# First layer of a four-layer gated network: ternary weights made during the routed experts, one stage from gather to transposed rows, and sums over partitions on TensorE

## Chip, core and metric

The kernel runs on one core of one Trainium2 chip. The metric is the device time of one execution in microseconds (us). Three executions of the kernel before took 3488.2, 3493.2 and 3496.24 us; the median is 3493.2 us.

## What is computed

Four layers, each an attention-like part and a feed-forward part, both added to the rows x (2048 tokens of 512 numbers) behind a layer norm and a tanh gate. The change touches layer 0 and two sums in layer 2's feed-forward part:

```python
# layer 0, "xattn": each token goes to one of four experts by its id; the context rows are the experts' weights
out = where(expert_ids == e, (silu(h @ Wg[e].T) * (h @ Wu[e].T)) @ Wd[e].T, out)
x = x + tanh(g_xattn[0]) * out
# layer 0, ffn on _layernorm(x); for each of W_up, W_gate, W_down (2048x512 or 512x2048):
scale = mean(abs(w)) + 1e-8
q = clip(round(w / scale), -1, 1) * scale
x = x + tanh(g_ffn[0]) * ((silu(h @ wu.T) * (h @ wg.T)) @ wd.T)
# layer 2, ffn: per-tensor fp8 scale of the rows and of the hidden values
scale_x = maximum(max(abs(x2d)) / 448, 1e-6)
```

All three expert matrices are the same context rows here, so a tile needs two products, one with the turned context for gate and up together and one for down.

## The kernel before

The kernel is a sequence of stages (`stage`). In a stage each engine runs its own instruction list in order, the order in which it is written, and waits on semaphores that other engines or DMAs raise; a stage ends with all of its engines at a barrier. Nothing overlaps across a stage's end but DMAs that nobody waits for. P is 128 partitions, T is 16 row tiles of 128 tokens, D is 512, F is 2048, A (`ROUTED`) is 19.

Layer 0 runs through these stages:

1. `routed_context` turns the context into `cT` (fp16 high and low parts), sorts the tokens by expert into 19 tiles of 128 and starts the first four gathers of x rows.
2. `experts`, loops over the 19 tiles (a or i). Per tile: GpSimd gathers 128 rows of x (L482) into a ring of four; VectorE takes statistics (L647, L649, L651), GpSimd the root (L533), VectorE normalises (L658), ScalarE and VectorE split into fp16 high and low parts (L619, L663); TensorE turns them (L568), VectorE copies them out of PSUM (L670); TensorE multiplies by the context (L578, 12 matmuls); ScalarE silu (L628), VectorE product (L693), ScalarE high part (L632), GpSimd low part (L538); TensorE turns (L587), VectorE copies (L677, `copy_hidden`), TensorE multiplies again (L596, 12 matmuls), ScalarE scales the result (L640) and SP stores it to `expert_rows` in DRAM (L521). SP has issued the load of all of x (4 MB) and the store of `cT` (4 MB) at the start. GpSimd's order in step i is root(i+3), low part(i), gather(i+4). VectorE's is `copy_rows`(i+1), product(i), normalise(i+2), statistics(i+3), low part(i+2), `copy_hidden`(i-1). After the last tile GpSimd gathers the 16 tiles of results back in token order (L555) and VectorE adds them to x (L707).
3. `ternary_matrices`: 12 slabs of 1 MB (four of each matrix) are loaded (L743); VectorE sums absolute values (L759, then L765, L766), GpSimd adds over the partitions with `partition_all_reduce` (L750), VectorE makes the step size (L772 to L774), ScalarE scales and rounds to int32 (L816), VectorE clips to -1..1 in fp16 (L780), TensorE turns (L806), ScalarE copies to the matrices (L827, L830).
4. `scaled_gate`: one VectorE multiplication (L2921), a stage of its own.
5. `transposed_parts`: statistics of all 16 tiles (L159, L162, L164), roots (L172), then per tile normalise (L261), high part (L228), low part on GpSimd (L239), turn (L248), copy (L267).
6. `ternary_ffn`, whose first matmul is at L918. It prepares the matrices of later layers beside its matmuls and isn't changed.

Layer 2's feed-forward part: `fp8_rows` finds the largest absolute value of the normalised rows (L2384 per partition), GpSimd takes the maximum over partitions (L2371), and VectorE makes the scale (L2341 on). `fp8_ffn` does its first product once to find the largest hidden value (L2513, L2516, L2517), again with a GpSimd maximum (L2494), and VectorE makes the scale (L2521 to L2523); GpSimd then forms a root with `pow` (L2497) and a product (L2499), and only after that ScalarE starts on the second pass (L2484).

Of the kernel before, what the change touches and what calls it, by code (L numbers as in the profile page):

```python
# [25 lines left out]
P = 128  # L26
D = 512
# [459 lines left out]
def experts(k, cT, rows, rows_loaded, tokens, places, weights_of):  # L487
# [4 lines left out]
    UP, ROWS, HIDDEN, Y = (0, 1), 2, 3, (4, 5)  # L492
    YR, GR = 3, 8
    with stage(k, "x_loaded", "context_stored", "stats_ready", "mv_ready", "var_ready", "power_ready", "rstd_ready", "normal_ready",
               "hi_ready", "parts_ready", "rows_turned", "rows_copied", "up_ready", "silu_ready", "prod_ready",
               "hid_hi_ready", "hid_ready", "hid_turned", "hid_copied", "down_ready", "y_ready", "stored0", "stored1",
               "stored2", "got0", "got1", "got2", "got3", "got4", "got5", "got6", "got7", "added") as s:
        stored = (s.stored0, s.stored1, s.stored2)
        got = (s.got0, s.got1, s.got2, s.got3, s.got4, s.got5, s.got6, s.got7)
# [13 lines left out]
        got_y = s.sb("got_y", [P, GR, D], F32)  # L513

        @s.block.sync
        def _(sp):
            sp.dma_start(k.x[:], k.x_in.rearrange("(t p) d -> p t d", p=P)).then_inc(s.x_loaded, 16)
            sp.dma_start(k.context_parts, cT[:].rearrange("p l c n -> p (l c n)")).then_inc(s.context_stored, 16)
            for a in range(A):
                sp.wait_ge(s.y_ready, a + 1)  # L520
                sp.dma_start(k.expert_rows[cols(a, P), :], y[:, a % YR, :]).then_inc(stored[a % YR], 16)  # L521
            sp.wait_ge(s.context_stored, 16)

        @s.block.gpsimd
        def _(pool):
            pool.memset(power[:], -0.5).then_inc(s.power_ready, 1)
# [23 lines left out]
            for u in range(YR):  # L550
                pool.wait_ge(stored[u], 16 * len(range(u, A, YR)))
            for t in range(T):
                if t >= GR:
                    pool.wait_ge(s.added, t - GR + 1)
                pool.indirect_dma_start(out=got_y[:, t % GR, :], out_offset=None, in_=k.expert_rows,  # L555
                                        in_offset=bass.IndirectOffsetOnAxis(ap=places[:, t:t + 1], axis=0)
                                        ).then_inc(got[t % GR], 16)

        @s.block.tensor
        def _(pe):  # L560
# [38 lines left out]

            turn_rows(0)  # L600
# [11 lines left out]
        def _(act):  # L612
# [7 lines left out]

            high(0)
            high(1)
            for i in range(A + 2):
# [9 lines left out]
                if i + 2 < A:  # L633
                    high(i + 2)
# [2478 lines left out]
```

## Time and profile before

| | us |
|---|---|
| executions shown | 3488.2, 3493.2, 3496.24 |
| profiled execution, its own time | 3497.81 |
| its span | 3496.1 |
| mean granted TensorE clock | 0.89 of full |

| engine | busy us | share |
|---|---|---|
| TensorE matmul | 2737.5 | 78% |
| TensorE weight load | 1414.9 | 40% |
| VectorE | 2564.6 | 73% |
| ScalarE | 1847.2 | 53% |
| GpSimd | 715.6 | 20% |

The shares are means over some forty stages with different limits. The change is in the stages between 44 and 329 us and at two points near 2816 and 2921 us, so the lines of the trace there are read, not the shares.

### The profile page before, as it was taken

What the parts mean: (1) busy time and instruction counts of PE and PEld (TensorE: products, weight loads), DVE (VectorE), ACT (ScalarE), POOL (GpSimd) and SP (SyncE); (2) the same over time, 40 slices, a digit from 0 to 9 for tenths busy, and PEclk for the clock granted to TensorE, in tenths of its full rate; (3) what the DMA queues carried; (4) which work ended last, traced back from release to release, by engine and by line L of the source; (5) the groups of instructions that cost most, each with busy time, mean ns of one, the idle gap of its engine ahead of it and who ended that gap; (6) DMA issues with size and microseconds to landing.
All of it is one profiled execution on the core that took longest, in us unless ns stands there. A gap on an engine that the chain in (4) does not pass through costs nothing. (4 is left out here: it accounts for less than half of the span.)

```text
span 3496.1 us, 63537 instructions
## 1 busy us (share of the span) xinstructions
PE 2737.5 (78%) x21394; PEld 1414.9 (40%) x21394; DVE 2564.6 (73%) x4744; ACT 1847.2 (53%) x2674; POOL 715.6 (20%) x610
## 2 busy tenths in 40 slices
PE   5925999776799999999996677786788647758983
PEld 3413444333365656565663433343111323224541
DVE  5555667575799999999994666524699787986548
ACT  2324433233399999999992533322587222434551
POOL 4422000022101010010104233303012603550013
PEclk8965999897899999999998898897999769978996
DMA  5261431200000000000000200100331100023301
GB/s 172 73 207 49 145 103 61 100 0 16 18 8 12 13 7 13 7 13 7 7 1 15 85 0 0 58 17 13 85 78 32 55 15 1 0 66 65 65 6 53
DMA packets 65285, 151.90 MB, mean 43 GB/s; under 512 B 11793, under 2 KB 20001, under 8 KB 63329
## 3 DMA queue, kind: packets, MB, share of 16 engines
q1 hardware_dynamic: 62320, 140.43, 13.4%
q0 software_dynamic: 2800, 9.18, 0.9%
q8 instruction: 116, 1.90, 0.2%
q14 instruction: 49, 0.39, 0.0%
HBM read 93.61 MB, written 24.38 MB: 34 GB/s over the span
## 5 line engine op out<-in xcount | busy, mean ns | idle before, releaser
L1527 DVE TENSOR_REDUCE s_top<-ps 128x1 f32<-128x512 f32 x1024 | 657.4, 684 | 31.1 <-PE ps L1422 30.8
L1496 ACT ACTIVATE s_prob<-ps,s_shift,m_sq 128x1024 int16<-128x1024 f32 x512 | 614.7, 1201 | 30.6 <-DVE s_shift L1535 30.4
L1422 PE MATMUL ps<-s_ks,s_qs 128*128 128x512 f16 x1024 | 352.2, 385 | 62.3 <-issue 14.8
L1427 PEld LDWEIGHTS ps<-ident,s_prob 128*128 128x128 f16 x4096 | 272.5, 98 | 123.3 <-DVE m_o L1545 53.7
L1427 PE MATMUL ps<-ident,s_prob 128*128 128x128 f16 x4096 | 313.9, 220 | 0.7 <-ACT s_prob L1496 0.5
L1415 PE MATMUL ps<-s_ks,s_qs 128*128 128x512 f16 x1024 | 306.6, 381 | 0.7 <-ACT s_prob L1496 0.5
L1502 ACT ACTIVATE s_probT<-ps 128x1024 f16<-128x1024 int16 x256 | 261.9, 1023 | 5.6 <-PE ps L1427 5.1
L248 PE MATMUL ps<-ident,s_parts 128*128 128x128 f16 x768 | 93.3, 297 | 151.5 <-POOL s_parts L239 149.4
L1540 DVE CAST s_probT<-ps 128x1024 f16<-128x1024 int16 x256 | 174.4, 681 | 3.9 <-PE ps L1427 3.9
L2199 DVE TENSOR_SCALAR s_prob<-ps,s_cap 128x1024 f32<-128x1024 f32 x128 | 158.2, 1270 | 24.6 <-PE ps L2108 24.6
L1406 POOL TENSOR_TENSOR s_sums<-s_z 128x16 f32<-128x16 f32 x16 | 3.5, 217 | 835.5 <-DVE m_o L1545 835.5
L2804 DVE TENSOR_REDUCE s_ntop<-ps 128x1 f32<-128x512 f32 (+3 forms) x256 | 107.5, 484 | 86.7 <-PE ps L2664 86.7
L2143 ACT ACTIVATE s_prob<-s_prob 128x1024 f32<-128x1024 f32 x128 | 131.1, 1051 | 58.5 <-DVE s_prob L2199 55.5
L969 ACT ACTIVATE s_silu<-ps,scale 128x512 f32<-128x512 f32 x64 | 43.9, 685 | 206.8 <-PE ps L918 206.8
L1422 PEld LDWEIGHTS ps<-s_ks,s_qs 128*128 (+1 forms) x1024 | 80.2, 96 | 169.3 <-DVE s_top L1527 108.6
L2122 PE MATMUL ps<-s_prob,m_values 128*32 128x512 f32 x512 | 136.0, 610 | 12.8 <-ACT s_prob L2143 12.6
L1435 PE MATMUL ps<-s_hv,s_probT 128*128 128x32 f16 x4096 | 142.3, 176 | 1.7 <-ACT s_probT L1502 1.7
L228 ACT ACTIVATE s_parts<-s_rows 128x512 f16<-128x512 f32 x80 | 49.0, 627 | 178.1 <-DVE s_rows L261 150.2
L248 PEld LDWEIGHTS ps<-ident,s_parts 128*128 128x128 f16 x768 | 69.4, 134 | 177.7 <-POOL s_parts L239 177.7
L2125 PE MATMUL ps<-s_prob,s_ones 128*32 128x512 f32 x512 | 136.0, 610 | 0.0
L2775 ACT ACTIVATE s_prob<-ps 128x384 f32<-128x384 f32 (+1 forms) x192 | 89.6, 516 | 85.8 <-PE ps L2687 85.6
L1435 PEld LDWEIGHTS ps<-s_hv,s_probT 128*128 128x128 f16 x4096 | 129.5, 96 | 2.2 <-issue 2.2
(384 smaller groups left out, 6020.1 us busy)
## 6 DMA issues: line engine op xcount, KB each, us to landing
s_qs<-m_qT SPq DMA_DIRECT2D x144, 128.0 KB, 2.5
s_ks<-m_kT SPq DMA_DIRECT2D x96, 128.0 KB, 2.5
numbers<-s_numbers SPq DMA_DIRECT2D x21, 512.0 KB, 3.0
s_slabs<-numbers SPq DMA_DIRECT2D x21, 512.0 KB, 5.8
m_ks<-context_parts SPq DMA_DIRECT2D x12, 512.0 KB, 7.7
expert_rows<-s_y SPq DMA_DIRECT2D x19, 256.0 KB, 2.0
s_rows_in<-in_ctx SPq DMA_DIRECT2D x16, 256.0 KB, 3.0
x_sb<-in_x SPq DMA_DIRECT2D x1, 4096.0 KB, 14.4
```

The lines of the kernel that those rows point to most:

```text
L248: t = pe.transpose(k.ps16[:, u, cols(m, P)], parts[:, u, m // DC, cols(m % DC, P)], k.ident[:])
L1415: j = pe.matmul(pair(half)[:, m, :], qs[:, hb, bass.ds(t * P, P)], ks[:, hb, cols(2 * half + m, 512)], start=True, stop=True)
L1422: pe.matmul(quarter_at(q), qs[:, hb, bass.ds(t * P, P)], ks[:, hb, cols(q, 512)], start=True, stop=True).then_inc(s.top_scored, 1)
L1427: j = pe.transpose(turned(half, F16)[:, cols(m, P)], prob[:, u, cols(8 * half + m, P)].bitcast(F16), k.ident[:])
L1435: j = pe.matmul(output, probT[:, u, m, :], hv[:, hb, m, :], start=(m == 0), stop=(m == T - 1))
L1496: act.activation(prob[:, u, cols(half, HALF)], pair(half).rearrange("p m n -> p (m n)"), ACT.Exp, bias=shift[:, u:u + 1], scale=sq[:, bass ...
L1502: act.activation(probT[:, u, 8:16, :].rearrange("p m n -> p (m n)"), turned(1, I16), ACT.Copy).then_inc(s.half1_copied, 1)
L1527: dve.tensor_reduce(top4[:, u, q:q + 1], quarter_at(q), AX.X, ALU.max).then_inc(s.top_read, 1)
L1540: dve.tensor_copy(probT[:, u, 0:8, :].rearrange("p m n -> p (m n)"), turned(0, I16)).then_inc(s.half0_copied, 1)
L2122: pe.matmul(values_at(m)[cols(j, HD), :], values[:, b * KT + t, 2 * pair + j, :], prob[:, n % R, j, :], start=(t == 0), stop=(t == KT - 1))
L2125: i = pe.matmul(sums_at(m)[cols(j, HD), :], ones[:], prob[:, n % R, j, :], start=(t == 0), stop=(t == KT - 1))
L2199: dve.tensor_scalar(prob[:, n % R, :, :], k.ps[:, 2 * (n % A):2 * (n % A) + 2, :], cap[:, tile:tile + 1], -LIMIT, ALU.min, ALU.max).then_i ...
```

## The change

- `ternary_matrices` and `scaled_gate` are removed. The slabs are loaded, summed, scaled and clipped inside `experts`, into the tile `numbers` (fp16, not yet turned). x isn't loaded in `experts` any more: its place in memory and that of the later `hT` hold the slabs.
- In `experts` SP issues two slab loads in each of steps 0 to 2 and one in each of steps 7 to 12, and the store of `cT` in step 13. VectorE gets `clip`(i-7) and `absolute`(i-2) at the end of a step; ScalarE gets `multiply`(i-6) and takes `copy_hidden` over from VectorE, both at fixed places in its order. The sum over partitions is a matmul with a matrix of ones.
- Gathering back, adding, statistics, normalising and turning of the rows become one stage `expert_rows_added`, which works tile by tile, with the turning of the weights on TensorE and ScalarE in between. x is loaded there, in four pieces. Normalising moves from VectorE to ScalarE, the low part from GpSimd to VectorE.
- In `fp8_rows` and `fp8_ffn` the GpSimd maximum over partitions is replaced: VectorE spreads the column over 128 columns, TensorE turns it with an fp32 matmul by the identity, VectorE reduces the 128 columns. The sums in `ternary_ffn` stay on GpSimd.

In `experts`, SP's order:

```diff
-            sp.dma_start(k.x[:], k.x_in.rearrange("(t p) d -> p t d", p=P)).then_inc(s.x_loaded, 16)
-            sp.dma_start(k.context_parts, cT[:].rearrange("p l c n -> p (l c n)")).then_inc(s.context_stored, 16)
-            for a in range(A):
-                sp.wait_ge(s.y_ready, a + 1)
-                sp.dma_start(k.expert_rows[cols(a, P), :], y[:, a % YR, :]).then_inc(stored[a % YR], 16)
+            for i in range(A + 2):
+                if 1 <= i < A:
+                    sp.wait_ge(s.up_ready, i)
+                if i < NATS // 2:
+                    load(2 * i)
+                    load(2 * i + 1)
+                if NATS <= i - 1 < LAST:
+                    sp.wait_ge(s.scaled, i - NATS)
+                    load(i - 1)
+                if i == LAST + 1:
+                    sp.dma_start(k.context_parts, cT.rearrange("p l c n -> p (l c n)")).then_inc(s.context_stored, 16)
+                if i >= 2:
+                    sp.wait_ge(s.y_ready, i - 1)
+                    sp.dma_start(k.expert_rows[cols(i - 2, P), :], y[:, (i - 2) % YR, :]).then_inc(stored[(i - 2) % YR], 16)
```

TensorE's step (`add_up` waits for `sum_ready` and is a matmul of ones by one fp32 column) and ScalarE's step:

```diff
                 if i < A:
                     up(i)
+                if i % SLABS == 2 and 0 <= i // SLABS - 1 < M:
+                    add_up(i // SLABS - 1)
...
                 if i + 2 < A:
                     high(i + 2)
+                if 0 <= i - 6 < LAST:
+                    multiply(i - 6)
...
+                if 0 <= i - 1 < A:
+                    copy_hidden(i - 1)
```

VectorE's step, behind product(i) and again behind low(i+2):

```diff
+                if i % SLABS == 2 and 0 <= i // SLABS - 1 < M:
+                    step_size(i // SLABS - 1)
...
-                if 0 <= i - 1:
-                    copy_hidden(i - 1)
+                if 0 <= i - 7 < LAST:
+                    clip(i - 7)
+                if 0 <= i - 2 < LAST:
+                    absolute(i - 2)
+                if i % SLABS == 1 and 0 <= i // SLABS - 1 < M:
+                    partial_sum(i // SLABS - 1)
```

The new stage `expert_rows_added` (all lines are new; `GR` is 8, `R` is 4), GpSimd:

```python
            for t in range(GR):
                gather(t)
            pool.memset(power[:], -0.5).then_inc(s.power_ready, 1)
            pool.wait_ge(s.power_ready, 1)
            for t in range(T):
                pool.wait_ge(s.var_ready, t + 1)
                pool.tensor_tensor(k.rstd[:, t:t + 1], var[:, t:t + 1], power[:], ALU.pow).then_inc(s.rstd_ready, 1)
                if t + GR < T:
                    pool.wait_ge(s.added, t + 1)
                    gather(t + GR)
```

VectorE (`offset_of` waits for `rstd_ready`, `low` for `hi_ready`, `copy` for `turned`):

```python
            for t in range(T + 4):
                if t < T:
                    add(t)
                if 0 <= t - 3 < T:
                    low(t - 3)
                if t < T:
                    dve.wait_ge(s.added, t + 1)
                    dve.bn_stats(bn[:, t, :], k.x[:, t, :]).then_inc(s.stats_ready, 1)
                if 0 <= t - 4:
                    copy(t - 4)
                if 0 <= t - 1 < T:
                    offset_of(t - 1)
                if t < T:
                    dve.wait_ge(s.stats_ready, t + 1)
                    dve.bn_aggr(k.mv[:, t, :], bn[:, t, :]).then_inc(s.mv_ready, 1)
                    dve.wait_ge(s.mv_ready, t + 1)
                    dve.tensor_scalar(var[:, t:t + 1], k.mv[:, t, 1:2], LN_EPS, None, ALU.add).then_inc(s.var_ready, 1)
```

TensorE turns eight banks of weights (`turn_weights_of(0)`), then one bank and one tile of rows per step; ScalarE:

```python
            copy_weights_of(0)
            for t in range(T):
                copy_weights_of(t + 1)
                act.wait_ge(s.offset_ready, t + 1)
                if t >= R:
                    act.wait_ge(s.parts_ready, t - R + 1)
                act.activation(normal[:, t % R, :], k.x[:, t, :], ACT.Identity, bias=offset[:, t:t + 1],
                               scale=k.rstd[:, t:t + 1]).then_inc(s.normal_ready, 1)
                if t >= R:
                    act.wait_ge(s.turned, t - R + 1)
                act.wait_ge(s.normal_ready, t + 1)
                act.activation(parts[:, t % R, 0, :], normal[:, t % R, :], ACT.Copy).then_inc(s.hi_ready, 1)
```

In `fp8_rows` (in `fp8_ffn` the same with bank 7):

```diff
-            pool.partition_all_reduce(total[:], top[:], P, RMAX).then_inc(s.total_ready, 1)
...
+            dve.tensor_copy(wide_top[:], top[:].broadcast_to([P, P])).then_inc(s.spread, 1)
+            dve.wait_ge(s.total_ready, 1)
+            v.done(dve.tensor_reduce(total[:], k.ps[:, 3, 0:P], AX.X, ALU.max))
...
+            pe.wait_ge(s.spread, 1)
+            pe.matmul(k.ps[:, 3, 0:P], wide_top[:], k.ident32[:], start=True, stop=True).then_inc(s.total_ready, 1)
```

## Rows read from the trace of the kernel before

**Rows 1.** Experts' stretch: length; PE, PEld, DVE, ACT, POOL busy; clock; DMA share, GB/s

```profile
44.00:194.00 150.00, 126.53 (x760) 63.01 (x760) 76.51 (x152) 47.80 (x77) 53.57 (x54) 0.93 0.32 115
```

**Rows 2.** Timeline of one tile's round: start, duration, engine, line; [idle before <-releaser]

```profile
132.43 0.69 DVE L647 BATCH_NORM_STATS2 s_bn<-m_rows 128x6 f32<-128x512 f32 x1 [2.60 <-DMA m_rows<-in_x,m_tokens]
...
133.62 0.94 POOL L533 TENSOR_TENSOR s_rstd_e<-s_var_e,s_power 128x1 f32<-128x1 f32 x1 [3.52 <-DVE s_var_e L651]
...
135.86 1.00 POOL L482 DMA_INDIRECT m_rows<-in_x,m_tokens  x1 [0.17 <-issue]
...
139.26 0.69 DVE L647 BATCH_NORM_STATS2 s_bn<-m_rows 128x6 f32<-128x512 f32 x1 [1.52 <-DMA m_rows<-in_x,m_tokens]
```

**Rows 3.** Waits of the experts' stage (44 to 194 us): total, times, longest

```profile
DVE s_bn L647 <- DMA m_rows<-in_x,m_tokens: 43.3, 15, 5.6
```

**Rows 4.** Timeline: a gather beside two 4 MB transfers, and the last tile's statistics

```profile
62.61 1.01 POOL L482 DMA_INDIRECT m_rows<-in_x,m_tokens  x1 [0.16 <-issue]
...
69.00 0.69 DVE L647 BATCH_NORM_STATS2 s_bn<-m_rows 128x6 f32<-128x512 f32 x1 [5.61 <-DMA m_rows<-in_x,m_tokens]
...
168.01 0.69 DVE L647 BATCH_NORM_STATS2 s_bn<-m_rows 128x6 f32<-128x512 f32 x1 [3.08 <-DMA m_rows<-in_x,m_tokens]
```

**Rows 5.** Groups of instructions of the operations that move: count, busy, mean ns

```profile
L759 DVE TENSOR_REDUCE s_part<-m_nat 128x32 f32<-128x2048 f32 x12 | 27.4, 2279 | 9.4 <-DMA m_nat<-in_L_ffn_W_up 9.4
L780 DVE TENSOR_SCALAR s_tern<-s_whole 128x2048 f16<-128x2048 int32 x12 | 14.7, 1222 | 10.1 <-ACT s_whole L816 10.1
L816 ACT ACTIVATE s_whole<-m_nat,s_inv 128x2048 int32<-128x2048 f32 x12 | 24.0, 2010 | 49.3 <-DVE s_inv L774 49.3
L827 ACT ACTIVATE m_w_down<-ps 128x1024 f16<-128x1024 f16 x8 | 7.8, 1038 | 0.6 <-PE ps L806 0.6
L2271 ACT ACTIVATE s_norm<-s_delta,s_offset_d,s_factor_d 128x512 f32<-128x512 f32 x16 | 13.0, 814 | 39.7 <-DVE s_offset_d L2315 39.7
```

**Rows 6.** Timeline: TensorE at half clock, back to back at full clock, and after a gap

```profile
51.66 5.30 PE L578 MATMUL ps<-m_cT,s_hT 128*128 x12 [1.50 <-DVE s_hT L670]
...
127.43 0.62 PE L568 MATMUL ps<-ident,s_parts 128*128 128x128 f16 x8 [1.78 <-DVE s_parts L663]
128.03 4.45 PE L596 MATMUL ps<-m_cT,s_hidT 128*128 x12
...
135.80 2.75 PE L596 MATMUL ps<-m_cT,s_hidT 128*128 x12
...
141.88 2.75 PE L596 MATMUL ps<-m_cT,s_hidT 128*128 x12
```

**Rows 7.** Timeline: a VectorE operation that meets a GpSimd operation

```profile
172.46 1.16 POOL L538 TENSOR_TENSOR s_hid<-s_prod,s_hid 128x512 f16<-128x512 f32 x1 [1.19 <-ACT s_hid L632]
...
172.93 1.23 DVE L663 TENSOR_TENSOR s_parts<-s_normal,s_parts 128x512 f16<-128x512 f32 x1 [0.76 <-ACT s_parts L619]
```

**Rows 8.** Timeline: last result scaled, first and last gather back

```profile
192.86 0.69 ACT L640 ACTIVATE s_y<-ps,gate 128x512 f32<-128x512 f32 x1 [3.31 <-PE ps L596]
...
195.84 1.00 POOL L555 DMA_INDIRECT s_got_y<-expert_rows,m_places  x1 [10.34 <-DMA expert_rows<-s_y]
...
216.60 1.13 POOL L555 DMA_INDIRECT s_got_y<-expert_rows,m_places  x1 [0.30 <-issue]
```

**Rows 9.** Timeline: last copy of the turned rows, then the first matmul of `ternary_ffn`

```profile
327.09 0.69 DVE L267 COPY m_hT<-ps 128x1024 f16<-128x1024 f16 x1 [0.42 <-PE ps L248]
329.03 0.14 PEld L918 LDWEIGHTS ps<-m_hT,m_w_up 128*128 128x128 f16 x2 [2.25 <-DMA m_nat<-in_L_ffn_W_up]
```

**Rows 10.** Timeline in `fp8_ffn`: maximum found, scale found, GpSimd's root

```profile
2920.72 0.15 DVE L2517 TENSOR_SCALAR s_top<-s_top 128x1 f32<-128x1 f32 x1
...
2921.86 0.15 DVE L2523 TENSOR_SCALAR s_sh<-s_total 128x1 f32<-128x1 f32 x1
...
2928.41 0.59 POOL L2497 TENSOR_TENSOR s_root<-s_sh,s_power 128x1 f32<-128x1 f32 x1 [7.05 <-issue]
```

**Rows 11.** One line's durations, fp32 matmul by the identity (min/median/max ns)

```profile
L2871 PE MATMUL ps<-ident,s_ws_col x8: 421/421/581, 3457.1 to 3458.7; 128*128 128x128 f32 x8
```

More of the change, by code:

```diff
@@ L549, in _ @@
                     gather_rows(k, pool, rows, rows_loaded, tokens, i + ROWS_RING)
[L550 to L557, printed above, removed]
         @s.block.tensor
@@ L598, in down, with add_up @@
                 i.then_inc(s.down_ready, 1)
+            def add_up(m):
+                if m == 0:
+                    pe.wait_ge(s.ones_ready, 1)
+                pe.wait_ge(s.sum_ready, m + 1)
+                pe.matmul(k.ps[:, TOTAL, m:m + 1], ones[:], sums[:, m:m + 1], start=True, stop=True).then_inc(s.total_ready, 1)
             turn_rows(0)
@@ new lines, in turn_rows @@
+            def turn_rows(t):
+                pe.wait_ge(s.parts_ready, t + 1)
+                if t >= R:
+                    pe.wait_ge(s.copied, t - R + 1)
+                for m in range(2 * DC):
+                    i = pe.transpose(k.ps16[:, t % R, cols(m, P)], parts[:, t % R, m // DC, cols(m % DC, P)], k.ident[:])
+                i.then_inc(s.turned, 1)
+            turn_weights_of(0)
+            for t in range(T + 3):
+                if t < T:
+                    turn_weights_of(t + 1)
+                if t >= 3:
+                    turn_rows(t - 3)
@@ L2424, in fp8_ffn @@
 def fp8_ffn(k, xT, wfc, wproj, sx, sfc, sproj, gate):
-    with stage(k, "vsteps", "first_ready", "first_used", "max_ready", "total_ready", "scale_ready", "root_ready",
+    with stage(k, "vsteps", "first_ready", "first_used", "max_ready", "spread", "total_ready", "scale_ready", "root_ready",
                "power_ready", "a_ready", "relu_ready", "square_ready", "magic_ready", "sum_ready", "hid_ready",
@@ L2458, in _ @@
             pe.wait_ge(s.first_used, G * FC)
+            pe.wait_ge(s.spread, 1)
+            pe.matmul(k.ps[:, 7, 0:P], wide_top[:], k.ident32[:], start=True, stop=True).then_inc(s.total_ready, 1)
             with pe.Fori(0, G) as g:
@@ L2913, in _ @@
                     dve.tensor_tensor(x, x, y[:, u, :], ALU.add).then_inc(s.x_ready, 1)
-def scaled_gate(k, out, gate, scale):
-    with stage(k, "unused") as s:
-        @s.block.vector
-        def _(dve):
-            dve.tensor_tensor(out, k.gate[:, gate:gate + 1], scale, ALU.mult)
 def gated_layers(nc, inputs, out):
@@ L2971, in layer0_ffn @@
+        cT = wide[:, 0:2, :].rearrange("p l (c n) -> p l c n", c=DC)
         with memory(k) as sb2:
-            nats = [sb2("nat%d" % m, [P, F * D // P], F32) for m in range(2)]
-            ternary_matrices(k, matrices, k.scale, 0.0, 1e-8, nats)
-        scaled_gate(k, factor[:], 4, k.scale[:, 2:3])
-        hT = sb("hT", [P, 2, DC, N], F16)
-        transposed_parts(k, hT)
+            numbers = sb2("numbers", [P, 3 * SLABS_OF, SLAB], F16)
+            places = sb2("places", [P, T], I32)
+            with memory(k) as sb3:
+                rows = sb3("rows", [P, ROWS_RING, D], F32)
+                tokens = sb3("tokens", [P, ROUTED], I32)
+                weights_of = sb3("weights_of", [P, ROUTED], I32)
+                rows_loaded = [k.nc.alloc_semaphore("expert_rows_loaded%d" % u) for u in range(ROWS_RING)]
+                routed_context(k, cT, rows, rows_loaded, tokens, places, weights_of)
+                experts(k, cT, rows, rows_loaded, tokens, weights_of,
+                        (k.i.L0_ffn_W_up, k.i.L0_ffn_W_gate, k.i.L0_ffn_W_down), k.scale, numbers, hT)
+            expert_rows_added(k, places, hT, w, numbers, factor[:], k.scale[:, 2:3])
```

307 lines of the change are left out of this document (161 added, 146 removed).

## Prediction

> **What bounds the kernel now.** The change sits in layer 0 and at two points of layer 2's feed-forward part, so the timeline there is what matters, not the page's shares. Stages don't overlap; what is saved in one comes off the end, and four lengths have to be forecast.
>
> I read the experts' stage first. TensorE is busy 126.5 of 150 us and VectorE 76.5, which is 4.03 us of VectorE for each of 19 tiles [rows 1]. TensorE looks like the bound, but at full clock two of its products lie 6.08 us apart (135.80 to 141.88) [rows 6], while the statistics of tiles 4 and 18 start at 69.00 and 168.01: 14 rounds, 7.07 us each [rows 4]. The waits say why: VectorE sat 43.3 us, 15 times, for gathered rows [rows 3]. One round runs 132.43 statistics, 133.62 root on GpSimd, its low part, 135.86 gather issued, 139.26 next statistics: 6.83 us [rows 2]. This loop of VectorE, GpSimd and DMA sets the pace. VectorE's 2.9 us of waiting a tile (43.3/15) is the room for the new work; what counts is what the new work does to the loop.
>
> Behind it, the gather back starts at 195.84, 2.3 us after the last result (192.86 + 0.69) [rows 8], and the next matmul stage starts at 329.03 [rows 9]. From last result to first matmul: 135.5 us, in which the experts' engines do nothing but wait for one another.
>
> **Part 1: from the last result to the first matmul.** Removed are the gather back, `ternary_matrices`, `scaled_gate` and `transposed_parts`, 135.5 us. In their place: store and stage change, 2.3 + about 1.2 us, where the 1.2 is the stage change of [rows 9] (327.09 + 0.69 to 329.03 is 1.25), so 3.5; the new stage; another 1.25.
>
> The new stage step by step. GpSimd issues eight gathers before its first root. The 16 of before started at 195.84 to 216.60, 1.38 us apart [rows 8]: 11.1 us, then constant and root, about 1.4 (root 0.94 [rows 2]). VectorE's second step waits for it: 13 us in. x's four loads and the gathers are hidden beside that and are needed one after the other. Steps 2 and 3 are held by GpSimd, root 0.94, gather 1.00 and gaps of 0.17 to 0.3: 2.3 us each, 4.6. Then VectorE sets the pace: four wide and three small operations. In [rows 1, 2] six wide and two small ones fill 4.03 us though each wide one lasts 0.69, so a wide one costs about 0.6 and a small one about 0.17: 2.9 us, times 12, is 35. ScalarE has a bank copy 1.04, normalising 0.81 as L2271 [rows 5], and a high part of 0.6 (512 wide like the others, an estimate): 2.5 us, under it. TensorE turns 16 blocks a step; its half clock costs 0.11 us a block (12 wide products took 5.30 at half clock, a block is a quarter of one) [rows 6]: 1.8 us. GpSimd needs 2.3 until step 7. The drain of three more steps, with one high part, low part, turn and copy in a row, is 5. Sum 13 + 4.6 + 35 + 5 = 57.6, I take 58, between 55 and 68 (ScalarE's 2.5 with 0.8 us of round trips added in every step). Together 62.8 against 135.5: **72.7 us saved**, 63 to 76.
>
> **Part 2: the experts' stage gets longer.** VectorE loses `copy_hidden` (0.69) and gains a clip of 1.22 and a sum of 2.28 [rows 5]: 4.03 + 2.81 = 6.84 us a tile, just under 7.07. ScalarE, 47.8/19 = 2.5 us, gains a multiplication of 2.01 and a copy of 1.04 [rows 1, 5]: 5.6, covered. The sums in one pass are covered by the wait for rows. What isn't covered touches the loop:
>
> The clip (tiles 0 to 11, steps 7 to 18, gathers in steps 7 to 14) is issued just when GpSimd has the low part to make. In [rows 7] VectorE's operation, no wider than L647's of 0.69, began at 172.93 inside GpSimd's 172.46 to 173.62 and took 1.23: it waited for GpSimd to end. One of the two waits: if GpSimd does, the loop grows by the clip's 1.22 less the gap; if VectorE does, its 6.84 grows by 1.16. I take 1.15 us in eight steps, 9.2; bounds 0 and 13.
>
> The loads: six slabs of 1 MB in steps 7 to 12 are issued after the store of a result, as the gather is. A gather alone takes from 135.86 to 139.26, 3.4 us; the one issued at 62.61, with 8 MB in flight, 6.4 [rows 2, 4]. So 0 to 3.0 us a gather; a slab alone is less than 8 MB, I take 1.5, six times 9. The store of `cT` (4 MB), moved from the start to step 13, meets two gathers at 3.0 each, 6. The start gains nothing: four slabs are in flight when that gather at 62.61 is issued.
>
> The two partial sums and step sizes on VectorE's path cost about 0.5 us three times, the copy on ScalarE in the tail 0.35 twice: 2.2. Sum 9.2 + 9 + 6 + 2.2 = **26 us longer**; bounds 3, and 45 if each loop pays the full 3.0 and TensorE's clock falls too.
>
> Two rules of the Trainium skill speak to this part. Its page "SBUF — State Buffer", section "Who interferes with whom", says that a VectorE operation in a two-port mode and a GpSimd operation block each other fully and that `tensor_reduce` never does, and that a gather's descriptors are written by GpSimd through the same port. By it the clip costs up to 1.22 us a step and the sum nothing; [rows 7] shows the same lock with another operation. Its page "DMA: Bandwidth & Descriptors", section "Queues, rings and completion order", says each DMA engine takes turns between queues packet by packet. By that rule a gather would get half of the engines beside a load and lose well under the 3.0 us of [rows 4]; the six loads would then cost about 5 us and not 9.
>
> **Part 3: the two maxima.** In `fp8_ffn` the scale was ready at 2921.86 + 0.15, yet the root began at 2928.41, after 7.05 us of waiting for nothing that the trace shows, right behind the GpSimd maximum [rows 10]. Everywhere else a root follows its input in a few tenths (0.17 at 133.62) [rows 2]. I read this as the price of going from the special reduction back to ordinary code. Without it: spread copy 0.3, fp32 matmul 0.6 to 0.8 with its load (0.42 alone [rows 11]), reduction 0.3, three small steps 0.6, so the root starts about 2.2 us after 2920.87 in place of 7.5: 5.3 saved, and ScalarE's whole second pass moves with it. In `fp8_rows` the new way costs about 0.9 more and nothing waits for the old code. Together **4.4 us saved**; if the gap stays, 2 lost.
>
> The Trainium skill, page "GPSIMD Engine Reference", section "Instruction dispatch", says that the first call to freshly loaded GpSimd code pays about 6 us without an instruction in the profile; by that figure the saving would be 4.3 and not 5.3.
>
> **Rivals.** *A, the loop hides it all.* GpSimd wins the port and loads slip between gathers; the experts' stage grows by 5 us. For it: 2.9 us of waiting a tile. Against it: [rows 4, 7]. 21 us less than the forecast: 3421. *B, TensorE's clock falls in many tiles.* A TensorE wait of 1.78 us stood ahead of a product of 4.45 us in place of 2.75 [rows 6]; longer rounds make such waits the rule. 1.7 us in eleven tiles is 19: 3461. *C, slower than before.* The same taken to its end: TensorE stays at 1.2 GHz, two products of 5.30 and 16 turned blocks make a step of about 12.3 us (2 × 5.3 + 16 × 0.11). Over 19 tiles that is 100 us more, less the 77 saved: 3516. It decides from about 15 such tiles. Against it: a busier TensorE regained its clock in the next tile (135.80) [rows 6]. *D, the new stage doesn't pipeline.* Variance, root, offset, normalising, high part, low part form one chain; if it costs 4.2 us a tile, the stage has 20 us more: 3462. Against it: `low` trails by three steps and `copy` by four.
>
> **How the numbers follow.** -72.7 + 26 - 4.4 = -51 us. The profiled execution took 3497.8 us (span 3496.1), 4.6 above the median of the runs, so the difference is taken off the median: 3493.2 - 51 = 3442. Chances: forecast 0.51, A 0.22, B 0.13, D 0.08, C 0.04, no difference 0.02. A measurement can tell about 0.2%, 7 us. The range goes from A less 6 us of Part 1 to B and D plus 9: 3415 to 3470. Faster 0.94, same 0.02, slower 0.04.
>
> **What would show it.** Right: about 62 us from last result to first matmul; statistics 7 us apart up to tile 9, over 8 from step 7 on, with longer GpSimd or VectorE operations at the clip; longer gathers in steps 7 to 14; the root in `fp8_ffn` within 1 us of its scale. Wrong: rounds still at 6.9 in steps 7 to 12 (A), TensorE at half clock in most tiles (B, C), more than 3.3 us a tile in the new stage (D), or a GpSimd gap that has only moved.

## The result, and the profile after

The changed kernel takes 3442.9 us, the median of four runs (3437.6 to 3446.8), against 3493.7 us before: a ratio of 0.985, 95% interval 0.9838 to 0.9862. The forecast was 3442, the range 3415 to 3470. The profiled execution took 3446.8 us with a span of 3445.1, which is 51.0 us below the span of before.

Four stretches make up the difference. They are read in the same order as in the prediction.

**The experts' stage.** Here is the stretch from its first statistics to its last result (length; busy time of PE, PEld, DVE, ACT, POOL; clock; DMA share, GB/s), then the rows of its waits (total, times, longest):

```profile
44.00:218.00 174.00, 129.78 (x766) 66.16 (x766) 105.94 (x169) 85.54 (x108) 59.52 (x55) 0.89 0.41 147
```

```profile
DVE s_bn L698 <- DMA m_rows<-in_x,m_tokens: 30.5, 12, 7.9
PE ps L629 <- DVE s_sums L733: 21.1, 3, 11.7
```

VectorE's and ScalarE's work has grown by 29 and 38 us [rows 1]. VectorE's wait for gathered rows has shrunk from 43.3 to 30.5 us [rows 3], so part of the new work did go into it. The second wait was in no step of the prediction: TensorE stands 21 us, in three pieces, before the matmul that adds up a matrix's partial sums.

The timeline of VectorE's statistics (L698, L647 before) shows where the rounds get longer. These are the starts for tiles 4, 9, 10, 16 and 18:

```profile
68.91 0.69 DVE L698 BATCH_NORM_STATS2 s_bn<-m_rows 128x6 f32<-128x512 f32 x1 [5.95 <-DMA m_rows<-in_x,m_tokens]
...
104.43 0.69 DVE L698 BATCH_NORM_STATS2 s_bn<-m_rows 128x6 f32<-128x512 f32 x1
...
114.24 0.69 DVE L698 BATCH_NORM_STATS2 s_bn<-m_rows 128x6 f32<-128x512 f32 x1 [3.05 <-DMA m_rows<-in_x,m_tokens]
...
172.53 0.69 DVE L698 BATCH_NORM_STATS2 s_bn<-m_rows 128x6 f32<-128x512 f32 x1 [7.93 <-DMA m_rows<-in_x,m_tokens]
...
189.45 0.69 DVE L698 BATCH_NORM_STATS2 s_bn<-m_rows 128x6 f32<-128x512 f32 x1 [0.41 <-DMA m_rows<-in_x,m_tokens]
```

From tile 4 to 9 a round takes 7.1 us as before (35.5 / 5). From 9 to 18 it takes 9.4 (85.0 / 9). The longest, 14.6 us, ends at 172.53: its gather was issued at 161.93, 1.9 us behind the 4 MB store of `cT` at 160.06. Over 14 rounds the mean is 8.61 us against 7.07 [rows 4].

GpSimd in a step without and in a step with the clip (L567 root, L572 low part, L482 gather, L743 clip):

```profile
97.60 0.94 POOL L567 TENSOR_TENSOR s_rstd_e<-s_var_e,s_power 128x1 f32<-128x1 f32 x1 [3.63 <-DVE s_var_e L702]
98.53 1.14 POOL L572 TENSOR_TENSOR s_hid<-s_prod,s_hid 128x512 f16<-128x512 f32 x1
99.84 1.00 POOL L482 DMA_INDIRECT m_rows<-in_x,m_tokens  x1 [0.17 <-issue]
...
115.43 1.68 POOL L567 TENSOR_TENSOR s_rstd_e<-s_var_e,s_power 128x1 f32<-128x1 f32 x1 [6.57 <-DVE s_var_e L702]
116.35 1.74 POOL L572 TENSOR_TENSOR s_hid<-s_prod,s_hid 128x512 f16<-128x512 f32 x1
118.25 1.00 POOL L482 DMA_INDIRECT m_rows<-in_x,m_tokens  x1 [0.16 <-issue]
```

```profile
115.85 1.22 DVE L743 TENSOR_SCALAR m_numbers<-m_hT 128x2048 f16<-128x2048 int32 x1
```

The clip keeps its 1.22 us and GpSimd's two operations grow by 0.74 and 0.60. But the two grow over the same stretch of time: from the root's start to the gather it is 2.24 us without and 2.82 with the clip, 0.58 more.

The matmul L629 and what follows on TensorE:

```profile
136.83 0.59 PE L629 MATMUL ps<-s_sums,s_ones 128*128 128x1 f32 x2 [5.95 <-DVE s_sums L733]
137.28 1.01 PE L593 MATMUL ps<-ident,s_parts 128*128 128x128 f16 x8
138.08 4.54 PE L621 MATMUL ps<-m_w,s_hidT 128*128 x12
142.46 0.61 PE L612 MATMUL ps<-ident,s_hid 128*128 128x128 f16 x8
142.90 2.75 PE L603 MATMUL ps<-m_w,s_hT 128*128 x12
```

Behind the wait of 5.95 us the turning of the next rows is queued, then it and the product run at a granted clock of 0.50, which is 1.2 GHz (137 to 141.5 us; 4.54 us in place of 2.75 for twelve wide matmuls). The next product, at 142.90, takes 2.75 us again.

**The new stage.** The last result, the first add, the first root, ScalarE's copies and VectorE's stall after three steps, the last copy of turned rows, and the first matmul of the next stage:

```profile
216.62 0.69 ACT L689 ACTIVATE s_y<-ps,gate 128x512 f32<-128x512 f32 x1 [2.86 <-PE ps L621]
...
229.19 0.69 DVE L833 TENSOR_TENSOR x_sb<-x_sb,s_got_y 128x512 f32<-128x512 f32 x1 [8.18 <-DMA s_got_y<-expert_rows,m_places]
...
231.44 0.60 POOL L821 TENSOR_TENSOR rstd<-s_var,s_power 128x1 f32<-128x1 f32 x1
...
235.00 1.02 ACT L908 ACTIVATE m_w<-ps 128x1024 f16<-128x1024 f16 x1 [3.98 <-DMA x_sb<-in_L_ffn_W_gate]
...
238.88 0.69 DVE L842 TENSOR_TENSOR s_parts<-s_normal,s_parts 128x512 f16<-128x512 f32 x1 [3.81 <-ACT s_parts L923]
...
279.67 0.69 DVE L847 COPY m_hT<-ps 128x1024 f16<-128x1024 f16 x1 [0.53 <-PE ps L885]
...
281.41 10.79 PE L1007 MATMUL ps<-m_hT,m_w 128*128 128x512 f16 x41 [1.78 <-PEq L104]
```

From the last result (217.31) to the first matmul: 64.1 us, against 135.5 before [rows 8, 9].

**The second maximum.** The maximum, the scale, GpSimd's root and ScalarE's first operation in `fp8_ffn`:

```profile
2868.89 0.15 DVE L2607 TENSOR_SCALAR s_top<-s_top 128x1 f32<-128x1 f32 x1
...
2870.73 0.15 DVE L2616 TENSOR_SCALAR s_sh<-s_total 128x1 f32<-128x1 f32 x1
...
2871.04 0.56 POOL L2587 TENSOR_TENSOR s_root<-s_sh,s_power 128x1 f32<-128x1 f32 x1 [64.26 <-DVE s_sh L2616]
...
2872.05 0.60 ACT L2576 ACTIVATE s_relu<-ps 128x512 f32<-128x512 f32 x1 [64.09 <-POOL s_root L2589]
```

The root starts 2.2 us after the maximum in place of 7.7, and the gap of 7.05 us [rows 10] is gone. In `fp8_rows` the scale starts 1.65 us after the start of the maximum L2465 (2762.95 to 2764.60), before it was 0.72: 0.93 more.

### The profile page after: what moved, and what is told of

It is laid out like the page before. It is cut to its first block and busy times, and to the rows that moved or that the text cites. A ratio compares the mean times of both kernels' runs of the same rounds, so it can differ in the third digit from the quotient of the medians.

```text
span 3445.1 us, 63421 instructions
## 1 busy us (share of the span) xinstructions
PE 2739.6 (80%) x21404; PEld 1417.0 (41%) x21404; DVE 2552.2 (74%) x4757; ACT 1874.1 (54%) x2709; POOL 706.1 (20%) x602
## 5 line engine op out<-in xcount | busy, mean ns | idle before, releaser
L1516 PEld LDWEIGHTS ps<-ident,s_prob 128*128 128x128 f16 x4096 | 272.7, 98 | 123.4 <-DVE m_o L1634 52.2
L1007 PE MATMUL ps<-m_hT,m_w 128*128 128x512 f16 x1024 | 231.9, 381 | 1.8 <-PEq L104 1.8
L248 PE MATMUL ps<-ident,s_parts 128*128 128x128 f16 x640 | 76.4, 293 | 129.1 <-POOL s_parts L239 127.3
L1007 PEld LDWEIGHTS ps<-m_hT,m_w 128*128 128x128 f16 x1024 | 100.5, 98 | 124.0 <-issue 2.4
```

Source lines behind the costliest of these rows:

```text
L1007: i = pe.matmul(k.ps[:, 2 * (n % 2) + j, :], wt[:, c, cols(n, P)], hT[:, l, c, cols(g, GT)], start=(l == c == 0), stop=(l == 1 and c == DC ...
L1516: j = pe.transpose(turned(half, F16)[:, cols(m, P)], prob[:, u, cols(8 * half + m, P)].bitcast(F16), k.ident[:])
```

## The experiments

One measure serves for all of the experts' stage: from the statistics of tile 4 to the start of the last result's scaling. It is 147.7 us in the kernel after (68.91 to 216.62). Three runs below leave this stage alone and give 147.3, 147.3 and 146.8, so its mean is 147.3 and half a microsecond can be read from it. Before the change it was 123.9 and, in a second trace with the same stage, 124.2. The excess to explain is 23.3 us. The time of a whole run, at 0.13% either way, can't tell single terms of 3 to 7 us; where it is given it is as a check.

**The clip.**

```diff
-                act.activation(whole[:, g % 2, :], nat(g), ACT.Copy, scale=inv[:, m:m + 1])
+                act.activation(numbers[:, g, :], nat(g), ACT.Copy, scale=inv[:, m:m + 1])
...
-                dve.tensor_scalar(numbers[:, g, :], whole[:, g % 2, :], 1.0, -1.0, ALU.min, ALU.max
+                dve.tensor_scalar(numbers[:, g, 0:1], numbers[:, g, 0:1], 1.0, -1.0, ALU.min, ALU.max
```

> The kernel after with the clip of the twelve slabs cut to one column, and ScalarE writing its scaled slab straight as 16-bit numbers (so the rounding and the clip of the first layer's ternary matrices are left out). Everything else stays: loads, sums, scaling, turning. It prices the clip, its 1.22 us on VectorE and what it does to GpSimd's root and low half beside it. The forecast's own term: the lock holds GpSimd 1.15 us in 8 steps, so the experts' stage ends about 9 us earlier than in the kernel after (217.3 us, last result there). The reading of the trace of after: root and low half grow by 0.74 and 0.6 us but the gather is issued only about 0.6 us later, and three of those rounds end in another wait, so about 3 to 5 us. A third: the loop is bound by the landing of the rows while slabs load, and the clip is hidden behind it, so 0 to 1 us.

The measure falls to 143.6 us: 3.7 for the clip, lock and VectorE's own time together. The whole is 3442.9 us (ratio 0.9853, 0.9837 to 0.9869), which can't show it. GpSimd in the same step as above, now without the clip:

```profile
115.58 0.94 POOL L567 TENSOR_TENSOR s_rstd_e<-s_var_e,s_power 128x1 f32<-128x1 f32 x1 [6.65 <-DVE s_var_e L702]
116.50 1.15 POOL L572 TENSOR_TENSOR s_hid<-s_prod,s_hid 128x512 f16<-128x512 f32 x1
117.82 1.00 POOL L482 DMA_INDIRECT m_rows<-in_x,m_tokens  x1 [0.17 <-issue]
```

Root and low part are back at 0.94 and 1.15 us and the gather comes after 2.24 us. So the lengthening is the clip's. It makes the gather 0.58 us late in a step, half of the 1.15 of the forecast; the 3.7 us of the measure are 0.46 for each of the eight gathers that have a clip beside them.

**The slab loads.**

```diff
-                if NATS <= i - 1 < LAST:
-                    sp.wait_ge(s.scaled, i - NATS)
-                    load(i - 1)
...
-                dve.wait_ge(nat_loaded[g % NATS], 16 * (g // NATS + 1))
+                dve.wait_ge(nat_loaded[g % NATS], 16)
```

> The kernel after with the six slab loads of steps 7 to 12 left out, so that the second half of the twelve slabs is made from the first six that stay in place (part of two of the ternary matrices is then wrong data). It prices the sharing of the DMA engines between slab loads and the gathers of rows. The forecast's own term: 1.5 us in each of six steps, 9 us off the end of the experts' stage (217.3 us in the kernel after). The reading of the trace of after: with a slab beside it a gather needs 5.5 us from issue to the statistics in place of 3.4, in about five rounds that wait for it, so 10 to 12 us. A rule by which each packet takes its turn would give the load more than half of the engines in that time, and no less than that. If neither: under 3 us, since VectorE is held by its own added work in those rounds anyway (round of 7.3 us or more without the wait for rows).

The measure falls to 140.9 us: 6.4, or 1.1 a load (whole: 3437.9 us, ratio 0.9836, 0.9822 to 0.985). My reading of the landings alone (5.5 against 3.4 us, 10 to 12 in all) was too high, since in some of these rounds VectorE came late for the rows anyway (in the kernel after, the statistics at 140.29 us waited for none).

**The store.**

```diff
-                if i == LAST + 1:
+                if i == A - 2:
                     sp.dma_start(k.context_parts, cT.rearrange("p l c n -> p (l c n)")).then_inc(s.context_stored, 16)
```

> The kernel after with one line changed: the 4 MB store of the context's parts is issued in step 17 of the experts' loop, after the last gather of rows has been issued, in place of step 13. The forecast's own term: the store makes two gathers 3.0 us late each, so moving it gives back 6 us of the experts' stage. The reading of the trace of after: only one gather (161.9 us) is late, 10.6 us to its statistics in place of 3.8 to 5.5, so 5 to 7 us, all in one round. Against: the store then ends later than the last result and delays the stage's end (its 4 MB at about 400 GB/s are 10 us from about 185 us, so it should end by 200, before 210), or it falls on the gather of the last tile and gives nothing back.

The measure falls to 140.6 us: 6.7. The round of 14.6 us has become one of 7.5, and the stage's end doesn't wait for the store. The whole is 3439.1 us (ratio 0.9846, 0.9831 to 0.9861).

**The sum over the partitions.**

```diff
                 if i < A:
                     up(i)
-                if i % SLABS == 2 and 0 <= i // SLABS - 1 < M:
-                    add_up(i // SLABS - 1)
                 if i + 1 < A:
                     turn_rows(i + 1)
                 if 0 <= i - 2:
                     down(i - 2)
+                if i % SLABS == 2 and 0 <= i // SLABS - 1 < M:
+                    add_up(i // SLABS - 1)
...
-                if i % SLABS == 2 and 0 <= i // SLABS - 1 < M:
-                    step_size(i // SLABS - 1)
                 if i + 2 < A:
                     normalise(i + 2)
...
                 if i + 2 < A:
                     low(i + 2)
+                if i % SLABS == 2 and 0 <= i // SLABS - 1 < M:
+                    step_size(i // SLABS - 1)
```

> The kernel after with TensorE's matmul that adds up a matrix's partial sums over the partitions put after the down product of its step (and VectorE's two steps that read it after the low half), in place of between the up product and the turning of the next rows. It tests a cost that the forecast did not have: TensorE waits there for VectorE's partial sum, with the turning of rows queued behind (idle 3.5, 6.0 and 11.7 us before that matmul, the last beside the store). By that reading the three rounds shrink by 1 to 2 us each: 3 to 6 us off the stage. By the forecast, which gave these steps 0.5 us each on VectorE and no wait of TensorE: 0, as the order of work of VectorE is the same. The other side: the scale comes one product later, ScalarE's first scaling of each matrix waits for it with the copies behind it, 0 to 2 us slower.

TensorE at the first of the three (this kernel's timeline):

```profile
96.39 0.62 PE L593 MATMUL ps<-ident,s_parts 128*128 128x128 f16 x8 [0.27 <-DVE s_parts L714]
96.84 2.75 PE L621 MATMUL ps<-m_w,s_hidT 128*128 x12
99.43 0.28 PE L629 MATMUL ps<-s_sums,s_ones 128*128 128x1 f32 x2
99.57 0.61 PE L612 MATMUL ps<-ident,s_hid 128*128 128x128 f16 x8
```

The matmul no longer waits, and the product ahead of it runs in 2.75 us. The measure falls to 144.0 us: 3.3, so the order has a price (whole: 3441.4 us, ratio 0.9848, 0.9834 to 0.9862). But 3.3 is a net gain, and most of the 21.1 us of waiting has only moved. Over the stage TensorE's waits for the low parts of the rows (L593) grow from 15.1 to 24.5 us and those for ScalarE's copy of the hidden values (L621) from 4.0 to 13.0. Three of the latter are 3.17 us long, each behind ScalarE's first scaling of a matrix, as the expectation's other side had it.

The four add up to 20.1 of the 23.3 us. Each was taken out alone, so how far they overlap isn't known. What the other 3.2 are wasn't tried; the added work of VectorE and ScalarE that stays in all four kernels is the candidate.

**The loop itself.** If the round is set by the way through the gather, one more buffer for gathered rows should cut it, in the kernel before as well as after. The edit is the same in both:

```diff
-ROWS_RING = 4
+ROWS_RING = 5
```

> The kernel before with five buffers for the gathered rows in place of four: the forecast's claim on what bounds the experts' rounds, without the change. If it is the loop through the gather (3.4 us from issue to statistics in each round of 6.83 us), the 14 rounds from tile 4 (99.0 us) shrink towards what TensorE needs, 6.1 us a tile: 86 to 90 us, and the whole 9 to 13 us. If TensorE or VectorE bounds the rounds already, 97 to 99 us and no difference.

> The kernel after with five buffers for the gathered rows in place of four, so that a gather has a whole round of about 7 us between its issue and the statistics that read it (part of this memory was free). If the loop of statistics, root, low half, gather and statistics bounds the experts' stage, as the forecast has it, this cuts the loop: the rounds from tile 4 to tile 18 (120.5 us in the kernel after, 99.0 before the change) fall to what VectorE and TensorE need, 6.1 to 6.8 us where nothing is added and 7 to 8 with the added work, some 100 to 110 us; loads, store and lock, which cost about 6.4, 7.2 and 4.2 us of it, then hide almost all. Rival: the rounds are bound by VectorE's and GpSimd's own chain for a tile, and the gather only looks like the releaser: then 118 to 120 us.

In the kernel before, the 14 rounds take 84.4 us (63.51 to 147.88), 6.03 each, and the waits of that stretch list a single one for rows, of 0.9 us. Busy times from 75 to 147 us:

```profile
75.00:147.00 72.00, 72.00 (x478) 38.51 (x476) 45.70 (x96) 28.88 (x48) 35.79 (x35) 1.00 0.27 89
```

TensorE is busy all of the 72 us at full clock. The whole goes from 3497.7 to 3480.9 us (ratio 0.9947, 0.9934 to 0.9961), 17 us, more than the 9 to 13 expected: the round that ends with tile 4's statistics, beside the load of x and the store of `cT`, fell from 9.8 to 4.1 us too.

In the kernel after, the 14 rounds take 92.9 us (64.21 to 157.07), less than the 100 to 110 expected, and the whole is 3410.0 us (ratio 0.9752, 0.9739 to 0.9765). From 71 to 157 us:

```profile
71.00:157.00 86.00, 80.38 (x511) 42.02 (x510) 79.71 (x123) 57.11 (x72) 43.63 (x38) 0.98 0.57 204
```

and what this kernel's gathers and their wait looked like (landing from 75 to 188 us, min/median/max; wait from 44 to 186 us):

```profile
DMA to landing us min/median/max: 3.3/5.6/12.1
```

```profile
DVE s_bn L698 <- DMA m_rows<-in_x,m_tokens: 2.8, 2, 1.7
```

The gathers land as late as in the kernel after, up to 12.1 us beside the store, and hardly anyone waits: 2.8 us in all. Now VectorE (busy 79.7 of 86 us) and TensorE (80.4) both have little left. The expectation was too high in its 7 to 8 us for a round with added work: 11 of the 14 rounds took 4.7 to 7.1 us, and only the other three took 7.4, 8.8 and 9.6.

Between these two kernels the change is worth 70.9 us (3480.9 to 3410.0), 20 more than between before and after: the new work lengthens the measure from 111.1 to 120.8 us only, 9.7 in place of 23.3.

**The start of the new stage.**

```diff
             for q in range(4):
+                if q:
+                    sp.wait_ge(s.added, 4 * q - 3)
                 sp.dma_start(k.x[:, cols(q, 4), :], rows_of[:, cols(q, 4), :]).then_inc(x_loaded[q], 16)
...
-            for t in range(GR):
-                gather(t)
             pool.memset(power[:], -0.5).then_inc(s.power_ready, 1)
             pool.wait_ge(s.power_ready, 1)
+            for t in range(4):
+                gather(t)
             for t in range(T):
                 pool.wait_ge(s.var_ready, t + 1)
                 pool.tensor_tensor(k.rstd[:, t:t + 1], var[:, t:t + 1], power[:], ALU.pow).then_inc(s.rstd_ready, 1)
-                if t + GR < T:
-                    pool.wait_ge(s.added, t + 1)
-                    gather(t + GR)
+                if t + 4 < T:
+                    if t + 4 >= GR:
+                        pool.wait_ge(s.added, t + 5 - GR)
+                    gather(t + 4)
```

> The kernel after with only the edit of the new stage's start: loads two to four of x each wait until the tile three before their first has been added, the exponent's memset and four gathers stand ahead of the first root in place of eight gathers. In the kernel after, the first add waits until 229.2 us (8.2 us after the stage's start) with 4 MB of x and 2 MB of rows on the DMA engines at over 400 GB/s, and ScalarE's copies of turned weights stand still for 0.6, 1.8 and 4.0 us in the same stretch with their banks long turned. If both come from the shared DMA engines, last result to first matmul falls from 64.1 to 57 to 60 us and the stalls of ScalarE go. If the eight gathers ahead of the root hold the start (GpSimd issues one in 1.25 us), 60 to 62 us and the stalls stay. If the forecast's term of 13 us for the start was right as it stands (its gathers are needed anyway), 63 to 64.

ScalarE in this kernel:

```profile
220.82 8.36 ACT L911 ACTIVATE m_w<-ps 128x1024 f16<-128x1024 f16 x9 [4.58 <-PE ps L880]
230.41 0.81 ACT L921 ACTIVATE s_normal<-x_sb,s_offset,rstd 128x512 f32<-128x512 f32 x1 [1.24 <-DVE s_offset L840]
231.26 0.63 ACT L926 ACTIVATE s_parts<-s_normal 128x512 f16<-128x512 f32 x1
```

The nine copies run through in 8.4 us; in the kernel after they took from 221.89 to 237.5 with stalls of 0.6, 1.8 and 4.0 us and one of 0.45 among them. From last result to first matmul it is 59.2 us, as the first reading had it. The eight traces with the stage as it was give 60.8 to 65.2, mean 63.4, so the gain is about 4 us and not more than a little outside their spread; the whole (3442.9 us, ratio 0.9845, 0.9831 to 0.9858) doesn't show it.

That the stalls come from the bytes in flight is not shown, and one run speaks against it. The kernel with five buffers (`ring5`) has this stage unchanged, with all four loads and eight gathers issued at its start, and its nine copies run through as well:

```profile
190.28 8.36 ACT L908 ACTIVATE m_w<-ps 128x1024 f16<-128x1024 f16 x9 [4.58 <-PE ps L877]
```

While they did, the DMA engines moved 374 and 395 GB/s (194 to 196 and 196 to 198 us); in the kernel after it was 375 and 389 in the stretch in which the stalls begin (224 to 226 and 226 to 228). The other seven traces with the stage unchanged have the stalls, in sizes of 0.4 to 4.7 us. From last result to first matmul the kernel with five buffers takes 60.8 us, so beside a stage without stalls the edit is worth 1.6 us and not 4. What ScalarE was waiting for stays open: its banks had been turned, and the releasers that the trace names, TensorE and a slab load of the stage before, had long been done. The two halves of the edit weren't tried apart.

**The GpSimd reduction.** Two kernels put one back into `fp8_ffn`, with a result that nobody reads. The first:

```diff
             pool.memset(power[:], -0.5).then_inc(s.power_ready, 1)
+            pool.wait_ge(s.max_ready, 1)
+            pool.partition_all_reduce(idle[:], top[:], P, RMAX)
             pool.wait_ge(s.power_ready, 1)
```

> The kernel after with the GpSimd reduction over the partitions put back into the fp8 stage of the last layer, ahead of GpSimd's root, but with a result that nobody reads; the maximum still comes from TensorE. It tells what the 7 us were that ScalarE waited after the reduction in the kernel before. If going back to ordinary code behind that reduction is what costs (the forecast), the 5.5 us come back although no one waits for the reduction's result: maximum to ScalarE's first square 8 to 9 us in place of 3.0. If it was the reduction's own latency, or the wait for its result, 3.0 to 3.7 us.

```profile
2867.87 0.38 POOL L2587 PARTITION_ALL_REDUCE s_idle<-s_top  x1 [63.02 <-DVE s_top L2610]
2876.03 0.59 POOL L2590 TENSOR_TENSOR s_root<-s_sh,s_power 128x1 f32<-128x1 f32 x1 [7.78 <-issue]
```

The scale was ready at 2869.6 us, yet the root starts at 2876.03, and ScalarE 9.5 us after the maximum (2867.58 to 2877.08) in place of 3.2. The gap is there although no one reads the reduction (whole: 3445.7 us, ratio 0.9857, 0.9842 to 0.9872). The second:

```diff
             pool.wait_ge(s.power_ready, 1)
+            pool.partition_all_reduce(idle[:], power[:], P, RMAX)
             pool.wait_ge(s.scale_ready, 1)
```

> As the run before it, but the unread reduction is of a constant and is issued at the stage's start, some 50 us or more before the root, so GpSimd sits waiting between the two. If the code that the root needs is fetched when the root's turn comes, the 5.5 us come back here too (8 to 9 us from the maximum to ScalarE's first square). If it is fetched as soon as the reduction is done, while GpSimd waits, 3.0 us as in the kernel after. The forecast did not say which; the second seems likelier, since the queue stands at a wait right behind the reduction.

```profile
2808.67 0.10 POOL L2585 MEMSET s_power<- 128x1 f32 x1 [57.91 <-POOLq L104]
2814.34 0.38 POOL L2587 PARTITION_ALL_REDUCE s_idle<-s_power  x1 [5.57 <-issue]
2873.46 0.60 POOL L2589 TENSOR_TENSOR s_root<-s_sh,s_power 128x1 f32<-128x1 f32 x1 [58.75 <-DVE s_sh L2618]
```

Here the root follows its scale (2873.22 + 0.15) within 0.1 us and ScalarE starts 3.2 us after the maximum (2871.37 to 2874.52). The price is paid while GpSimd waits, as the second reading had it (whole: 3444.9 us, ratio 0.9859, 0.9843 to 0.9874). The switch into the reduction has a price too: 5.57 us between memset and reduction, with nothing to wait for. In the kernel before this first price isn't seen: GpSimd stood 62.47 us at the wait for the maximum and the reduction then started 0.1 us behind it (2920.98).

**The third part alone**, `fp8_rows` and `fp8_ffn` of the kernel after put into the kernel before (their functions are in the diff of the change):

> The kernel before with only the change's third part: both fp8 stages sum over the partitions on TensorE. The forecast's terms: 5.3 us saved in the last stage and 0.9 lost in the stage ahead of it, together 4.4 us, 3489 us. If the gap stays for another reason, 2 us slower, 3495.5.

3491.7 us (ratio 0.9991, 0.9982 to 1.0), 2.6 less than the 3494.3 of before in the same comparison. The interval holds the 4.4 of the forecast, but it reaches 1.0 as well, so the whole time rules out the loss of 2 us and doesn't prove the gain. In its trace ScalarE starts 3.2 us after the maximum (2923.19 to 2926.36).

**Together**: the store late, the sum late, the start of the new stage and five buffers.

> The kernel after with four edits together: the store of the context's parts in step 17, the sum over the partitions after the down product, five buffers for the rows, and in the new stage the second to fourth load of x each issued when the tile three before its first is added, with four gathers ahead of the first root in place of eight. By the rows of the runs so far the first two are worth 7.2 and 2.7 us of the rounds and overlap with the third, so the rounds from tile 4 to 18 come to 98 to 104 us in place of 120.5; the start of the new stage gets 4 to 6 us shorter: 20 to 26 us in all, 3417 to 3423 us. If the first rows of the new stage do not wait for the shared DMA engines, its part is 0 and it is 3422 to 3428; if the gather is not the loop's end, 3428 to 3432.

3406.8 us (ratio 0.9742, 0.9729 to 0.9756), 10 us below the expected 3417 to 3423 since the rounds took 91.1 us and not 98 to 104. It is the fastest kernel of this study: 36 us below the kernel after, of which five buffers alone give 33. The measure is 119.1 us (62.63 to 181.77), and 59.2 us pass from last result to first matmul. Store and sum, worth 10 us with four buffers, bring under 2 with five (rounds 91.1 against 92.9 us).

## Why the prediction was right, point by point

**What bounds the kernel.** Right, and shown by `before_ring5`: with the way through the gather cut, the round falls from 7.07 to 6.03 us, at TensorE's 6.08 [rows 6].

**Part 1, 72.7 us saved.** 71.4 measured (135.5 - 64.1). Result to stage 3.5 as forecast (217.31 to 220.84). VectorE's second step after 11.4 us, not 13. Steps in steady state 2.8 us, not 2.9. The first add waited 8.18 us for its rows, but that was hidden as forecast: the first root (231.44) followed GpSimd's eighth gather (230.29 + 0.95) and the memset, and its variance was ready at 231.00. Steps 2 and 3 were 1.74 us apart, not 2.3. What the sum had at nothing is ScalarE: with its stalls the nine bank copies lasted until 237.5, so the first normalised row came late and VectorE stood 3.81 us at 235.07. The drain took 6.3 us, not 5. In the prediction's order that is 11.4 + 4.4 + 3.8 + 33.6 + 6.3 = 59.5 us against 13 + 4.6 + 0 + 35 + 5. Errors of both signs nearly cancel, and that is luck.

**Part 2, 26 us longer.** 23.8 in this trace (193.55 to 217.31). Term by term, forecast against taken out:

| term | forecast | measured |
|---|---|---|
| clip against GpSimd | 9.2 | 3.7 |
| six slab loads | 9 | 6.4 |
| store of `cT` | 6 | 6.7 |
| sums, step sizes, ScalarE's copy | 2.2 | 3.3 (order of the sum alone) |
| not taken apart | - | 3.2 |

The clip was mis-sized most, by charging a whole blocked operation where the operation behind it was blocked over the same time. The store hit one gather for 6 to 7 us, not two for 3.0: the sum right, its parts not. The terms for the sums missed their mechanism: I counted VectorE's microseconds and not TensorE's queue behind the new wait, and the 3.3 us are what a better order gave back, not the whole price of the sums. The total is right within 3 us by luck: the two large terms were too high, and a missed one and an unexplained one made up for it.

On the two rules of the Trainium skill: in its page "SBUF — State Buffer", section "Who interferes with whom", the port is held for the whole instruction. That agrees with the low part, which takes 1.14 us alone and here ended 1.0 us after the clip did (116.35 + 1.74 against 115.85 + 1.22). By the rule of its page "DMA: Bandwidth & Descriptors", section "Queues, rings and completion order", the loads would, by the prediction's estimate, have cost about 5 us; 6.4 lies between that and the 9 of the forecast.

**Part 3, 4.4 us saved.** 4.6 by the traces: 5.57 saved (8.73 against 3.16 from maximum to ScalarE), 0.93 lost. The reading of the gap as the price of going back to ordinary code is borne out by `idle_reduce`, where no one waits for the reduction's result and the gap is there all the same. The Trainium skill, page "GPSIMD Engine Reference", section "Instruction dispatch", has about 6 us for the first call of freshly loaded code without an instruction in the profile. The 5.57 us ahead of the early reduction agree with it; the 7.78 behind the late one are longer, and so is the 7.05 of before [rows 10].

**The sum.** -71.4 + 23.8 - 4.6 = -52.2 us against -51.0 in the spans and -50.8 in the medians. The rest lies in stretches that the change doesn't touch: from the first matmul of `ternary_ffn` to the maximum in `fp8_rows` it is 2486.5 us before and 2481.5 after, and from ScalarE's start in `fp8_ffn` to the end 566.7 and 573.0. Over the thirteen traces of this study these two range over 7.4 and 6.3 us. So that the total came within 1 us of the forecast is luck; the terms were up to 5.5 us off and the comparison can't tell so little.

**The rivals.** A (the loop hides it all) didn't happen with four buffers, but its mechanism is there: with five buffers 9.7 us of added stage remain. B (the clock falls in many tiles) happened in the three tiles behind a partial sum and not in eleven. C (TensorE stays at 1.2 GHz) didn't: the granted clock of the stretch is 0.89, against 0.93 [rows 1]. D (the new stage doesn't pipeline) didn't: 2.8 us a tile.

## What to carry to other kernels

When work is put "into the slack" of a loop, first ask whether the slack is the loop's own latency. Here the same added work cost 23.3 us with four buffers in the ring and 9.7 with five, so the ring is lengthened first and the work added then. A matmul that reads another engine's late result belongs in TensorE's order where its wait has nothing urgent behind it, and a large store where no gather is on the path; with four buffers these two moves gave 3.3 and 6.7 us, with five together under 2. A blocked operation counts only for what it moves at the end of its chain.

## What the runs showed of the hardware that I had not expected

- A GpSimd reduction over partitions costs on both sides: 5.57 us ahead of it behind a memset, and 7.0 to 7.8 us after it when the next ordinary operation is wanted at once. If GpSimd sits at a semaphore in between, the second price is paid while it waits and nothing shows.
- In seven of the eight traces with the new stage unchanged ScalarE stood still for up to 4.7 us between copies whose inputs were ready, and TensorE behind it, while 4 MB of loads and 2 to 3 MB of gathers were in flight (375 to 417 GB/s in the kernel after). In the eighth (`ring5`), with the same transfers in flight, it did not. What stops it is open.
- A gather issued 1.9 us behind a 4 MB store landed after 10.6 us (162 to 172.5), where one alone takes 3.4; in the stretch with slab loads (104 to 173) the median was 5.5, and without them (`loads_off`, 75 to 188) 3.4.
